# Attention of the first of four blocks: the products with v move behind the scores, four transposed units follow in a row

## What is computed

```
q    = x @ q_w + q_b                              # 16 heads of 16
k, v = concat(ctx, x) @ kv_w + kv_b               # 512 keys
a    = softmax(where(mask, q k^T / 16, -inf))     # over the 512 keys
y    = (a v) @ out_w + out_b + x
h    = y * rsqrt(mean(y^2) + eps) * postnorm_w
x    = gelu(h @ w1 + b1) @ w2 + b2 + x            # 256 -> 1024 -> 256
```

## Time and profile before

| | |
|---|---|
| median of 3 runs | 1542.82 us (1542.89, 1538.76, 1542.82) |
| the profiled execution | 1538.59 us, span 1536.8 us, granted TensorE clock 0.998 |
| TensorE busy | 1467.4 us, 95% of the span |
| VectorE, ScalarE, GpSimd busy | 60%, 59%, 9% |
| first block's attention, first scores to the first gelu | 17.61 to 197.09 us |

### The profile page before, as it was taken

One profiled execution on the slowest core, in us unless ns is written; L12 is line 12 of the kernel. 1 busy time (PEld: TensorE's weight loads), 2 busy tenths in 40 slices (PEclk: granted clock), 3 DMA queues, 4 the chain that ended last, 5 costly groups with the idle time before them and its releaser, 6 DMA issues.

```text
span 1536.8 us, 28652 instructions
## 1 busy us (share of the span) xinstructions
PE 1467.4 (95%) x9824; PEld 1131.2 (74%) x9824; DVE 914.9 (60%) x3306; ACT 902.3 (59%) x2807; POOL 140.9 (9%) x171
## 2 busy tenths in 40 slices
PE   7999999999999999999999999999899988999996
PEld 5766688878787878687878787778666666866664
DVE  4777722445454545545545545531999995178887
ACT  5878933434444434443444444433899997289996
POOL 2010011000000000100000000011222222022200
PEclk9999999999999999999999999999999999999999
DMA  7000103010010100101001000000100100000000
GB/s 295 2 2 1 39 26 124 1 41 23 1 63 1 48 16 1 64 0 49 15 1 64 1 1 0 1 0 1 56 2 9 36 15 8 1 1 9 22 2 15
DMA packets 10879, 40.66 MB, mean 26 GB/s; under 512 B 2416, under 2 KB 2672, under 8 KB 8688
## 3 DMA queue, kind: packets, MB, share of 16 engines
q1 hardware_dynamic: 10736, 38.82, 7.0%
HBM read 37.77 MB, written 1.05 MB: 25 GB/s over the span
## 4 chain that ended last, share of the span: by engine, by line
PE 66%; ACT 16%; DVE 4%; issue 3%; DVEq 0%; POOLq 0%; ACTq 0%; POOL 0%
ACT probs L980 10%; PE bank L809 7%; PE bank L790 7%; PE bank L823 7%; PE bank L782 7%; PE bank L769 7%; PE bank L772 7%; PE bank L749 5%; PE bank L738 5%; ACT pT L988 4%; PE bank L798 4%; PE bank L583 2%; PE bank L567 2%; DVE probs L1245 2%; DVE probs L1227 1%
## 5 line engine op out<-in xcount | busy, mean ns | idle before, releaser
L980 ACT ACTIVATE probs<-probs,negmax 128x256 f32<-128x256 f32 (+1 forms) x640 | 349.4, 559 | 44.1 <-DVE negmax L1245 43.6
L1061 ACT ACTIVATE pT<-bank 128x512 f32<-128x512 f32 x128 | 76.5, 597 | 387.8 <-PE bank L798 387.8
L583 PEld LDWEIGHTS bank<-ident,probs 128*128 128x128 f32 x1536 | 167.4, 141 | 120.6 <-ACT probs L980 61.8
L583 PE MATMUL bank<-ident,probs 128*128 128x128 f32 x1536 | 226.0, 280 | 30.8 <-ACT pT L988 19.8
L1390 DVE TENSOR_REDUCE stats<-bank 128x1 f32<-128x257 f32 x256 | 108.5, 425 | 212.1 <-PE bank L790 211.1
L1245 DVE CUSTOM_DVE_ANT_0 probs<-bank,mask_a 128x256 f32<-128x256 f32 (+1 forms) x384 | 174.1, 508 | 31.2 <-PE bank L567 26.5
L988 ACT ACTIVATE pT<-bank 128x512 f32<-128x512 f32 x288 | 171.2, 596 | 9.6 <-PE bank L583 9.5
L809 PE MATMUL bank<-pT,probs 128*128 128x256 f32 x512 | 132.7, 381 | 2.7 <-ACT pT L1061 2.7
L790 PE MATMUL bank<-kT,pT 128*128 128x257 f32 x512 | 132.7, 382 | 0.6 <-ACT pT L1044 0.6
L980 ACT ACTIVATION_READ_ACCUMULATOR probs<-probs,negmax 128x1 f32 x640 | 133.1, 208 | 0.0
L1052 ACT ACTIVATE probs<-bank,stats 128x257 f32<-128x257 f32 x256 | 118.7, 474 | 3.5 <-DVE stats L1393 3.5
(11 more groups left out here) (111 smaller groups left out, 2489.4 us busy)
## 6 DMA issues: line engine op xcount, KB each, us to landing
w_m<-in_w SPq DMA_DIRECT2D x6, 1024.0 KB, 7.4
g_qkv<-in_g SPq DMA_DIRECT2D x4, 1536.0 KB, 7.5
q_res<-in_g SPq DMA_DIRECT2D x4, 1536.0 KB, 6.8
w_qkv<-in_w SPq DMA_DIRECT2D x3, 768.0 KB, 4.4
g_bv<-in_gbv SPq DMA_DIRECT2D x8, 256.0 KB, 7.1
g_o<-in_go SPq DMA_DIRECT2D x4, 512.0 KB, 3.4
q_res<-in_go SPq DMA_DIRECT2D x4, 512.0 KB, 3.4
rows<-in_rows SPq DMA_DIRECT2D x1, 1664.0 KB, 14.1
```

The source lines that it names most:

```text
L583: last = nc.tensor.transpose(out[:, n * P:(n + 1) * P], probs[:, u % PROBS, q * T + t * P:q * T + (t + 1) * P], ident[:, :])
L980: last = nc.scalar.activation(s, s, ACT.Exp, bias=negmax[:, u % PROBS, k:k + 1], scale=-1.0, accum_out=sums[:, tile % 2, q, j * c.res + r: ...
```

## The change

- `times_v` of the first block goes to slot 4 vq + 12 instead of + 10: into the first slot of a quad, and there behind the scores and ahead of everything else. From quad 3 on, a quad is now scores, products with v, four units of transposes.
- `norm_slot` counts 8 slots from y's slot instead of 6. y's own slot is counted from `pv_slot`, so it moves by 2, and the normed rows by 4. The change of `norm_slot` shifts nothing in the fourth block, whose normed rows `normed` leaves out.
- k1, v0 and v1 of the next part start in slots 16, 25 and 29 of a part instead of 14, 22 and 26.
- At the border the table is shifted: the transposes of slots `count`+2 and +3 and the last but one `times_v` come behind the first f, the last `times_v` with its reciprocals is moved from f = 2 to f = 4, where y follows at once.
- ScalarE's first MLP waits for the last but one `times_v` before its first gelu.

```
     def pv_slot(self, vq):
-        return QUAD * vq + 10
+        return QUAD * vq + (10 if self.host else 12)
...
     def norm_slot(self, p):
-        return self.y_slot(p) + (10 if self.kinds == "mult" else 6)
+        return self.y_slot(p) + (10 if self.kinds == "mult" else 8)
...
-        at = [1, 4, 11] if self.kinds == "mult" else [2, 6, 14] if len(self.loads()) == 3 else [2, 6, 14, 22, 26]
+        at = [1, 4, 11] if self.kinds == "mult" else [2, 6, 14] if len(self.loads()) == 3 else [2, 6, 16, 25, 29]
...
                         scores(u)
+                    for vq in range(c.count // QUAD):
+                        if c.pv_slot(vq) == s and not c.host:
+                            times_v(vq)
...
                     for vq in range(c.count // QUAD):
-                        if c.pv_slot(vq) == s:
+                        if c.pv_slot(vq) == s and c.host:
                             times_v(vq)
...
-                            for s in {1: [2, 3], 2: [4, 5, 6], 4: range(7, 13),
-                                      8: range(13, c.last_slot() - c.count + 1)}.get(f, []):
+                            for s in {1: [2, 3, 4], 2: [5, 6], 4: range(7, 14),
+                                      8: range(14, c.last_slot() - c.count + 1)}.get(f, []):
...
             def mlp(n, gelu, before, own, keys=None):
                 st = S[f"m{n}"]
+                if n == 0:
+
+                    act.wait_ge(sem("a_pv"), S["a0"].at("a_pv", 0, SMALL[0].count // QUAD - 1))
```

## The result

The changed kernel takes 1548.35 us (median of 5 runs, 1547.73 to 1549.41), the kernel before 1538.96 us (5 runs, 1538.66 to 1542.89; two runs were added to the three shown above, and the median went from the upper to the lower of two groups). The ratio is 1.0053, with a 95% interval of 1.0038 to 1.0067: slower by 9.4 us. The two profiled executions differ by 1547.0 - 1536.8 = 10.2 us of span.

The account below looks back on a forecast made before the run. TensorE was taken to bound quads with projections, a scores-maximum-copy loop through VectorE the others. Quads +8.5 and border +2.1 made +10.6 us: 1549.2 from the profiled execution, 1553.4 as median; forecast's range 1548 to 1559, overall 1543 to 1560.

Parts of the forecast that it names:

- 3 us each way: Uncertainty for entering and leaving the products behind the scores: 0.1 us less or more in 29 quads.
- the other ends: Alternative estimate for quads without projections, 5.38 us instead of 5.30, adding 1.1 us to the total.
- Part 1: Products with v ahead of the transposes: VectorE's copy waits, delaying the next scores; quads without projections 0.87 us longer.
- The accident in quad 12: Kernel before: other work put the transposes 2.16 us behind the scores; the quad lasted 5.37 us.
- plain quad: A quad without projection matmuls: 4.43 us before, 5.30 us predicted with the change.
- The double buffer's 0.47: Quads of q and k0: third unit's transposes wait for the bank VectorE's copy empties, losing 0.47 us, giving 6.33.
- Two kinds of quad: Kernel before: quads with eight projection matmuls last 5.86 us, bound by TensorE; others 4.43, bound by a two-engine loop.
- the first rival: Changes of tile shape are what costs; one fewer per quad returns 9.6 us: +1.0, 1543.8 us, the same. Chance 0.13.
- The 0.02: Cost of entering the products from transposes: four transposes take 0.50 us, eight ahead of the products 1.02.
- Part 2: Moved slots: k1, v0, v1, y quads 5.86 us; v0 with reciprocals 6.08; behind y 6.10; normed rows 5.79.
- Part 3: Border to the MLP: y waits for the late last products with v and reciprocals; fifth f +2.1 us.
- The second and the third rival: Second: products overlap scores, faster, chance 0.08. Third: ScalarE's copies also wait, twelve more quads pay 5.6 us, chance 0.15.

Follow-up runs that it names:

- e4: Changed kernel with the products with v back between the second and third unit, in the same quad as with the change: 1533.88 us, ratio to the kernel before 0.9970.
- e2: Changed kernel with VectorE's copy one slot later, behind the second maximum instead of the first: 1541.81 us, ratio to the kernel before 1.0013.
- e3: Changed kernel with the last products with v and their reciprocals at f = 2 of the MLP, not f = 4: 1547.50 us, ratio to before 1.0059.
- e7: Kernel of e1 with the normed rows two slots later, at slot 52 instead of 50: 1542.06 us, ratio to the kernel before 1.0014.
- e6: Kernel of e4 with the border of e3 (last products with v and reciprocals at f = 2): 1535.19 us, ratio to the kernel before 0.9971.
- e5: Kernel of e6 with products with v behind the scores in the quads of k1, v0, v1 and y only: 1534.62 us, ratio to before 0.9970.
- e1: Kernel before with only the slots of k1, v0, v1 and normed rows moved, products with v at their old slots: 1544.37 us, ratio 1.0032.

## Why the prediction was right

The sign, the mechanism and the size held. I put the change at +10.6 us; the medians give +9.4 and the profiled executions +10.2. The time itself, 1553.4, was 5 us high because I carried the sum over to a median of three runs, of which two were high. The sum made against the profiled execution, 1549.2, is the one to compare: it took 1548.78. My own range for the forecast, 1548 to 1559, is wider than its terms: 3 us each way and 1.1 for the other ends give 1550.4 to 1557.5, and the median of 1548.35 lies under that.

- **Part 1, the loop.** The accident in quad 12 gave the price of late transposes, 5.30 for a plain quad, and 5.35 came. e4 takes the place of the products away and e2 the queue behind the copy; both move the plain quads as worked out. The double buffer's 0.47 in the quads of q and k0 came out within 0.01. "Two kinds of quad" was too few, though: before, k0's quads with reciprocals (9 and 17) last 6.31 us, with a wait of 0.18 for the copy. The sum is untouched, since its times before are whole stretches.
- **Part 1, the value taken for products behind the scores.** I took TensorE's work in a quad with projections as 5.86 either way. It is 5.71. This is the term that was mis-sized, by 0.15 us in 10 quads. It is the first rival at less than half its price, and only where TensorE is the bound: a change of tile shape fewer does save TensorE time. The timeline of k1's quad shows where, in the changed kernel:

```profile
40.33 1.03 PE L546 MATMUL bank<-hT,w_qkv 128*128 128x256 f32 x4
41.20 1.04 PE L583 MATMUL bank<-ident,probs 128*128 128x128 f32 x8
42.16 1.14 PE L567 MATMUL bank<-kT,q_res 32*128 32x512 f32 x8
```

and in e4:

```profile
38.27 1.03 PE L550 MATMUL bank<-hT,w_qkv 128*128 128x256 f32 x4
39.23 1.08 PE L621 MATMUL bank<-pT,v_two 128*32 128x128 f32 x32
40.24 1.09 PE L587 MATMUL bank<-ident,probs 128*128 128x128 f32 x8
41.27 1.14 PE L571 MATMUL bank<-kT,q_res 32*128 32x512 f32 x8
```

A projection group ahead of transposes lasts 0.87 us to the next start, ahead of the products 0.96; eight transposes last 0.96 behind a projection and 1.03 behind the products. The 0.02 that I read ahead of the products in the earlier trace rows was too low, since it set a group of eight behind scores against twice a group of four behind scores, and so counted the change out of the scores' shape twice. From full shape into the products costs 0.09 us (0.96 less 0.87) and back out 0.07 (1.03 less 0.96), together the 0.15 but for rounding. From the scores straight to the products no cost shows: they follow after 1.07 us (158.59 to 159.66), as the transposes do. The Trainium skill's rule (TensorEngine Tiling (Array Packing), Key Properties) is that changing the tiling mode drains TensorE. These rows agree in sign for the changes from and to the full shape, at below 0.1 us each, and show nothing for the third.
- **Part 2.** Behind y 5.88 for 6.10, the rest as stated or by the same 0.15. The sum of quads 2 to 30 was +8.5 by the prediction and +6.7 in the trace; 10 times 0.15 and 3 times 0.22 less, and 8 times 0.05 more for the plain quads, are the difference.
- **Part 3, the border.** +2.1 predicted, +2.4 measured, with the wait ahead of y 1.14 us; e3 returns 1.37. ScalarE's new wait cost nothing, as worked out: its first gelu follows at 203.12, and the products it waits for (201.06, 1.08 us) ended 1 us before.
- **What the sum had no term for:** the 1.9 us of the fourth block. What the sum was about, quads and border, came to 6.7 + 2.4 = +9.1 for +10.6, so part of the agreement of +10.6 with +10.2 is luck: the 1.9 make up for what I took too much in the quads.
- The second and the third rival fell: the transposes follow the scores after 2.08 us and not after 1.71 or less (1.07 + 0.64), and no quad with the projections at the later slots lost the 0.47.

## What to carry to other kernels

Before moving work ahead of an instruction, list who waits for that instruction and what is queued behind the waiter; a copy that "waits for nothing" may do so only because its producer comes first in a loop through two engines. An accident in the old trace, a place where something else delays the same instruction, can price such a move: here it gave 5.30 us for 5.35. And a change that loses as a whole can hide a gain: here its slots were worth 5 us and the place of the products cost 12.

## What the runs showed of the hardware

The granted clock falls to its lower level, 1.2 GHz, for some 3.4 us at a time (6 us x 0.28 x 2 in each window below; in e7's quad 12 for twice that, 80 to 90 us), and how often differs between executions and kernels. The windows of the changed kernel around three such falls, all in the fourth block, columns as above:

```profile
1421.00:1427.00 6.00, 4.88 (x38) 3.69 (x42) 5.69 (x31) 3.60 (x14) 0.00 (x0) 0.72 0.00 0
1465.00:1471.00 6.00, 4.38 (x32) 3.48 (x32) 5.58 (x28) 3.59 (x14) 0.00 (x0) 0.72 0.13 48
1510.00:1516.00 6.00, 5.11 (x44) 3.32 (x45) 4.88 (x24) 4.76 (x17) 0.00 (x0) 0.72 0.12 44
```

and the kernel before, at the same work as the first and the second of them (its only fall of that length):

```profile
1410.00:1416.00 6.00, 4.18 (x50) 3.00 (x50) 5.86 (x26) 4.65 (x17) 0.72 (x1) 1.00 0.01 3
1456.00:1463.00 7.00, 5.80 (x49) 4.17 (x49) 6.70 (x35) 4.60 (x18) 0.00 (x0) 0.76 0.12 42
```

Three falls against one there, and 1.9 us more for the same instructions. The other traces bear this out. From the first scores of the fourth block to the end of the span, by the number of such falls in it (the fall that every one has when TensorE is done left out):

| falls | executions | us |
|---|---|---|
| 0 | e6 | 184.8 |
| 1 | e3, e4, e5, e7, before | 185.4, 185.7, 185.9, 185.9, 185.9 |
| 2 | e1 | 186.7 |
| 3 | e2, the changed kernel | 187.8, 187.8 |

Some 1 us a fall there. Between the border (the fifth f) and the fourth block the same instructions take 1148.3 to 1148.6 us in the three executions without a fall (the changed kernel, e4, before), and with one 1149.2 (e1, e2), 1150.4 (e3), 1150.6 (e5) and 1151.5 (e6, clock 0.83 over 624 to 634 us): 0.6 to 3.2 us for one fall. e7 has two there and takes 1150.6. Whether the change itself brings its falls is open: its five runs have clocks of 0.995 to 0.997, while 12 of the 18 runs of the kernel before beside e1 to e4 have 0.998.

In e1 and e7 a fall came in quad 12, behind a quad in which TensorE had waited for VectorE twice, in e1 for 1.17 and 1.03 us; the scores then took 2.09 us for 1.14:

```profile
80.28 1.35 PE L583 MATMUL bank<-ident,probs 128*128 128x128 f32 x8 [1.17 <-DVE pT L1253]
82.67 2.09 PE L567 MATMUL bank<-kT,q_res 32*128 32x512 f32 x8 [1.03 <-DVE negmax L1245]
```

The matmuls of the kernel before wait there for 1.17 us alone, and there is no fall. But two waits are not enough: it waits in quad 27 for 0.79 and 0.94 us, and e1 in quad 19 for 0.79 and 0.96, and no fall follows. e7's ten runs follow their mean clock: 1539.62 to 1539.81 us at 0.998, 1543.01 to 1543.94 at 0.994. So the scatter of some 4 us between runs of one kernel goes with the clock, and gains of 1 us like e3's and e6's drown in it. What makes the clock fall in one place and not in another was not tried, and stays open.
